# VectorE without its wait for the gather issues of GpSimd, in the first stage of a two-layer graph network

## The reference, cut to what matters

```
ego  = x @ W1.T + b1
neigh = segment_sum(edge_weight[:, None] * x[src], dst)      # layer 0
out  = leaky(ego + (neigh + neigh * x) @ W2.T + b2)
x    = layernorm(x + out / norm(out))
e    = relu(edge_attr @ ee_w1 + ee_b1) @ ee_w2 + ee_b2       # layer 1
h    = (1 + eps) * x + segment_sum(x[src] + e, dst)
h    = relu(ln(h @ w1 + b1)); h = relu(ln(h @ w2 + b2)); y = h @ w3 + b3
x    = layernorm(x + relu(ln(x + y)))
```

## Time and profile before

| | us |
|---|---|
| three runs | 1132.07, 1132.28, 1135.72 |
| their median | 1132.28 |
| the profiled execution | 1133.75 |
| its span | 1131.9 |
| granted TensorE clock in it, mean | 0.994 |
| busy in the span: PE, DVE, ACT, POOL | 1079.9, 987.4, 687.3, 802.4 |

### The profile page before, as it was taken

One profiled execution on the slowest core, in us unless ns is written; L12 is line 12 of the kernel. 1 busy time (PEld: TensorE's weight loads), 2 busy tenths in 40 slices (PEclk: granted clock), 3 DMA queues, 4 the chain that ended last, 5 costly groups with the idle time before them and its releaser, 6 DMA issues.

```text
span 1131.9 us, 21235 instructions
## 1 busy us (share of the span) xinstructions
PE 1079.9 (95%) x5297; PEld 893.0 (79%) x5297; DVE 987.4 (87%) x2795; ACT 687.3 (61%) x1677; POOL 802.4 (71%) x840
## 2 busy tenths in 40 slices
PE   6899999999999999999899999999999999999996
PEld 4788777777777777777677888888888888888875
DVE  6999999999999999999987888888888888888865
ACT  4577777787777777667644455445545554554453
POOL 7777777777777777777677777777777777777610
PEclk9999999999999999999999999999999999999998
DMA  8457767767766656667877777777777777777620
GB/s 236 139 157 203 204 191 204 207 189 204 207 192 185 180 169 178 189 176 206 279 210 218 209 218 212 218 220 219 209 217 224 211 213 222 222 210 216 204 74 12
DMA packets 106088, 222.13 MB, mean 196 GB/s; under 512 B 20003, under 2 KB 57369, under 8 KB 106010
## 3 DMA queue, kind: packets, MB, share of 16 engines
q0 software_dynamic: 53408, 164.16, 50.8%
q1 hardware_dynamic: 52602, 57.11, 16.1%
HBM read 203.96 MB, written 17.23 MB: 195 GB/s over the span
## 4 chain that ended last, share of the span: by engine, by line
PE 65%; DVE 12%; POOL 9%; issue 8%; DMA 4%; ACT 1%; POOLq 0%; DVEq 0%; ACTq 0%
PE ps_z L1405 28%; POOL raw L990 8%; PE ps_e L1128 7%; PE ps_s L1349 6%; PE ps_y L1405 6%; PE ps_sum L1133 4%; PE ps_sum L1135 4%; DVE msg L2182 4%; PE ps_tr L1474 3%; DVE msg L2188 3%; DVE oh L225 3%; DMA raw<-in_x,src_all 3%; PE ps_w L1228 2%; PE ps_y L1354 1%; POOL grow L1051 1%
## 5 line engine op out<-in xcount | busy, mean ns | idle before, releaser
L1051 POOL DMA_INDIRECT grow<-table_dram,src_all x401 | 389.0, 970 | 144.1 <-issue 118.2
L990 POOL DMA_INDIRECT raw<-in_x,src_all x399 | 378.6, 949 | 121.5 <-issue 102.7
L1405 PE MATMUL ps_z<-w_high,a 128*128 128x512 f32 x784 | 252.4, 393 | 0.5 <-DVE a L2545 0.5
L1128 PE MATMUL ps_e<-we,attr 65*128 65x256 f32 x832 | 225.0, 392 | 14.4 <-DVE msg L2188 12.8
L1133 PE MATMUL ps_sum<-msg,oh 128*128 128x512 f32 x464 | 227.6, 491 | 7.4 <-DVE msg L2188 6.6
L1677 ACT ACTIVATE msg<-raw,w_sb 128x256 fp32r<-128x256 f32 x416 | 193.5, 499 | 53.9 <-DMA raw<-in_x,src_all 45.9
L225 DVE TENSOR_SCALAR oh<-lane,rel 128x128 fp32r<-128x128 f32 x871 | 211.6, 302 | 16.7 <-DMA raw<-in_x,src_all 16.6
L1128 PEld LDWEIGHTS ps_e<-we,attr 65*128 65x128 f32 x832 | 152.8, 193 | 57.3 <-issue 34.3
L2182 DVE SCALAR_TENSOR_TENSOR msg<-raw,w_sb,msg 128x256 fp32r<-128x256 f32 x416 | 182.0, 474 | 8.7 <-ACT msg L1680 8.3
L1135 PE MATMUL ps_sum<-msg,oh 128*128 128x512 f32 x464 | 184.0, 397 | 0.0
L1908 ACT ACTIVATE aF<-ps_tr,be,g 128x128 f32<-128x128 f32 x392 | 149.6, 464 | 37.9 <-PE ps_tr L1474 35.7
(11 more groups left out here) (189 smaller groups left out, 1559.5 us busy)
## 6 DMA issues: line engine op xcount, KB each, us to landing
attr<-in_attrT SPq DMA_DIRECT2D x50, 192.0 KB, 4.0
raw<-in_x,src_all POOLq DMA_INDIRECT x416, 3.1
grow<-table_dram,src_all POOLq DMA_INDIRECT x401, 3.8
w_raw<-in_m_w SPq DMA_DIRECT2D x48, 128.0 KB, 3.7
table_dram<-table SPq DMA_DIRECT2D x23, 256.0 KB, 2.8
attr<-in_attrT SPq DMA_DIRECT2D x24, 160.0 KB, 4.2
xs<-in_x SPq DMA_DIRECT2D x24, 128.0 KB
xTb<-in_xT SPq DMA_DIRECT2D x24, 128.0 KB, 2.6
```

Of the source, the lines that this page charges most:

```text
L990: pool.indirect_dma_start(out=raw[:, j, :], out_offset=None, in_=x, in_offset=bass.IndirectOffsetOnAxis(ap=src_all[:, q * TILES + j:q * TI ...
L1051: pool.indirect_dma_start(out=grow[:, j, :].bitcast(F32), out_offset=None, in_=table_dram, in_offset=bass.IndirectOffsetOnAxis(ap=src_all[ ...
L1128: mm = pe.matmul(ps_e[k % 3][:, (j - j0) * D:(j - j0 + 1) * D], attr[:, j * P:(j + 1) * P], we1[:, :], start=True, stop=True)
L1405: mm = pe.matmul(acc, left[a], right[b], start=False, stop=stop and a == 1, skip_group_check=True)
```

## The change

`issued` is no longer allocated, the gathers of the first stage no longer raise it, and `follow` with its call is gone. Nothing else is different: each engine has the same instructions in the same order, and every wait on `high`, `summed`, `message`, `edge_net` and `gathered` stands where it stood.

```diff
-AHEAD = 4
@@ semaphores
-            issued = ma("issued")
@@ gpsimd, block 0 and near_gathers
                 pool.indirect_dma_start(
                     out=raw[:, j, :], out_offset=None, in_=x,
                     in_offset=bass.IndirectOffsetOnAxis(ap=src_all[:, j:j + 1], axis=0),
-                    engine_sem=issued,
                 ).then_inc(gathered[j], 16)
@@ vector
-            def follow(q, k):
-
-                tiles = TILES * q + PAIRS[k][0] + 2 + AHEAD
-                if not isinstance(q, int) or tiles <= TILES * (BLOCKS - 1) + LAST_TILES:
-                    dve.wait_ge(issued, tiles)
-
@@ near_block
                     j0, m = PAIRS[k]
-                    if has_pair(q, k):
-                        follow(q, k)
                     if s <= 5:
                         near_oh(path, b, s + 3)
```

More of the change, by code:

```diff
@@ L993, in near_gathers @@
                             ap=src_all[:, q * TILES + j:q * TILES + j + 1], axis=0),
-                        engine_sem=issued,
-                    ).then_inc(gathered[j], 16)
+                        ).then_inc(gathered[j], 16)
             def near_program(path):
```

## The result

The changed kernel took 1149.53 us (median of four runs, 1148.07 to 1150.78) against 1134.0 us of the kernel before on the same chips: a ratio of 1.0133, 95% interval 1.012 to 1.0145. That is 15 us slower, where 9 were forecast, and beyond the 1147 that the likeliest case had as its upper end. The profiled execution has a span of 1148.5 us instead of 1131.9. One run of the kernel before among the latter took 2766.59 us, for which the record has no cause, and is in none of the ratios.

What follows compares the result with a forecast made beforehand. GpSimd's gathers were taken to bound the first stage. Signal 0, wait 0 and stretched gathers +9 us summed to +9 us, moving the median from 1132.3 to 1141.3 us, with a range of 1132 to 1150.

Steps and rivals of the forecast that it cites:

- the likeliest case: First-stage gathers stretched as summed, +4 to +15 us, giving 1136 to 1147 us; chance 0.66.
- GpSimd's gathers set the first stage's pace: First stage: 0.946 us a gather plus 0.305 us gap, 21.25 us a block; anything added shifts the second stage whole.
- The signal costs nothing: First-stage gathers raising the signal: second-stage gathers without it have the same gap, so its removal was taken as 0.
- Another operation on SBUF alone: VectorE work besides L2182 claimed to hold up a gather starting inside it until it ends, at most 0.4 us each.
- part 3: VectorE's remaining waits: `high` catches it once a block, then it drifts forward by up to 0.74 us in sum.
- One or two stretches of 0.1 to 0.25 us a block, and one of the tail: First-stage gathers lengthened by VectorE's drift: 0.3 to 0.6 us a block, 6 to 12 us over the held stretch.
- part 4: Cost of VectorE's drift, as gathers start inside L2182 or the tail: 9 us taken, 0.44 us a block.
- The rate of 24 ns a gather: Extra length of unheld second-stage gathers, 970 against 946 ns; for 351 first-stage gathers 8.4 us.
- many stretches (over +15): Rival: a stretched gather on every second pair, 1.1 us a block, 23 us in all, 1155 us; chance 0.08.
- the case that was summed: Terms 0 + 0 + 9 = +9 us from stretched first-stage gathers; +4 to +15 us had chance 0.66.
- the phase holds by itself: Rival: `high` catches VectorE at every pair, so gathers stay unstretched, 1131.4 to 1132.3 us; chance 0.13.
- only the one-hots: Rival: only one-hots hold a gather, two a block by 0.07 us, 2.9 us, 1135.2; chance 0.10 with few stretches.

Runs made afterwards that it cites:

- idle_wait: Kernel before with AHEAD = -4 instead of 4, so signal and wait instruction stay but the wait never holds VectorE: 1147.92 us, ratio 1.0129.
- psum_operand: Changed kernel (no wait) with L2182's third operand read from PSUM instead of SBUF, low halves of the output not the reference's: 1136.19 us, ratio 1.0013.
- psum_operand_wait: Kernel before, with its wait, and L2182's third operand read from PSUM, low halves not the reference's: 1134.36 us, ratio 1.0021.
- ahead_5: Kernel before with AHEAD = 5 instead of 4, VectorE held one gather (1.25 us) later: 1138.57 us, ratio 1.0048.

## Why the prediction was off

- *GpSimd's gathers set the first stage's pace, and what is added to them shifts the second stage whole*: right. The gaps of 0.305 us that stay as they are show the first, and the last column above the second.
- *The signal costs nothing, and nothing comes from VectorE's earlier start*: right; the gap stayed at 0.305 us, and idle_wait, which keeps the signal, lost as much as the changed kernel within their intervals.
- *A gather is stretched when it starts inside L2182, not inside L2188*: right, and psum_operand shows the operand to be the reason. "Another operation on SBUF alone" was too wide (bn doesn't hold one), "at most 0.4 us a piece" too small (0.88 us at most), and one-hots that a gather starts in do hold it, by 67 ns on average.
- *`high` takes the place of the removed wait*: right in kind, wrong in number, and this is the step that failed, in part 3: I read one catch at 312.96 and let VectorE be caught there once a block, with the phase it had before, and drift from there by its own slack. In the changed kernel VectorE idles ahead of 68 of the 180 pairs of 60 to 499 us, and at 52 of them, 2.6 of every nine, the profile names ScalarE's L1676. ScalarE, now early as well, waits for the landings (92.6 us in 110 to 490, before 34.4), and these come 2.7 to 5.7 us after a gather's issue, a wide spread beside the tenth of a microsecond that the phase would have to hold. By tenths of a microsecond around the nearest gather's start, 178 of the 186 pairs of the kernel before begin their L2182 at 0.15 to 0.25 us; of the 180 of the changed kernel no tenth between -0.65 and +0.65 holds more than 21. The phase is not a slow drift from one anchor, it is near to even.
- *One or two stretches of 0.1 to 0.25 us a block, and one of the tail*: the mis-sized term of part 4, which follows from that step. Measured are 103 stretched gathers of 338, 5.2 a block, of 0.16 us on average: 0.83 us a block where I had 0.44, and 18.3 us for the stage where I had 9. With the phase taken as even, an estimate from the rows of before comes near to this: a pair of L2182 is 0.87 us of the 2.5 us of two gathers, so 0.35 x 17 = 5.9 gathers a block would start in one, and with holds of 0 to 0.3 us, 0.15 in the middle, this is 0.9 us a block. It is made with hindsight and right in part by luck, as in the trace only 61 of the 103 start in an L2178, 36 in a one-hot and 6 in the tail.
- *The rate of 24 ns a gather*: I took it from the second stage because it was the longest unheld stretch. It was the wrong stretch: VectorE does other work there, and 172 of the 401 gathers start inside an instruction with a PSUM operand. The two short stretches gave 32 and 38 ns, nearer to the 49 measured, from 29 and 15 gathers.
- *The rivals.* The time that came, 15.5 us over the kernel before, lies in "many stretches (over +15)", which had 0.08, and not in the case that was summed. That the phase holds by itself has fallen. Of "only the one-hots" it can be said that they are a smaller part: what is left without L2182's is 16 of 49 ns, tail included. "Many stretches" names about the right count, 5.2 a block against 4.5, with too large a price for each.

The inference that I set against the rows, in "SBUF — State Buffer" of the Trainium skill, "Who interferes with whom", that descriptor generation needs the write interface and that an instruction with two SBUF inputs, which takes only the read interface, therefore didn't stall a DMA, is not borne out for these gathers: 66 gathers that began inside such an instruction took 10.5 us over the floor, and 74 inside the same one with a PSUM operand 0.2. The section's rule as such, that two SBUF inputs contend with a GpSimd instruction that reads SBUF, agrees with both, since in the kernel a gather's offsets are a column of `src_all`, an SBUF tile. No run here shows that it is this read that is held.

The gathers of all of the first stage that start inside a one-hot add up to 6.0 us in the changed kernel (47 of them over 966 ns) and to 1.4 us (24) in psum_operand. Most of the difference isn't the one-hots' own: six of the 47 are like the one of 67.22, held on into a pair of L2178, and take 3.3 us of the 6.0. The other 41 are held by 67 ns each, against 58 ns in psum_operand.

What stays open: why one-hots hold a gather and bn doesn't, which both read one tensor from SBUF; when a gather is held past one L2182 into the next; and how far GpSimd's own lateness, which gives VectorE more slack, feeds the loss. No run separates these.

## What to carry to other kernels

A wait that "holds an engine back for nothing" may be what sets its phase to another engine; before it is taken out, look at the duration of the other engine's instructions by stretch, not only at who waits. Where GpSimd issues indirect DMAs and is the bound, VectorE should be inside an instruction with a PSUM operand, or have just started a short one, when a gather begins; a wait put two short instructions too late was worse than none here. To size such a collision where nothing sets the phase, take it as even and count the share of the time in which a start would be caught, in the same mix of instructions.

## What the runs showed that I had not expected

- The same wait moved behind the one-hots of its pair turned from a gain of 15 us over no wait into a loss of 5 (1134, 1149.5, 1154.5 us).
- A gather's length is constant to a few ns when it isn't caught: 946, 946 and 947 ns on average over some 350 gathers in each of the three kernels that hold the phase (before, psum_operand_wait, ahead_5).
- Without the wait VectorE's own instructions are little shorter or longer (the one-hots' mean 302 to 297 ns, L2182's 474 to 481), so that the loss doesn't show in them; on VectorE's side there is only idle time that has moved from the one-hots to L2182 and grown.
